# Two graph layers on one core: node rounds of phase B in turns of six, with two spilled rounds among four kept ones, and a ring of three products

## The reference, cut to what matters

```python
def _L0(node_feature, W_l, W_r, edge_index):           # mean over neighbours
    summed = segment_sum(node_feature[src], dst, n)
    agg = summed / maximum(deg, 1.0)[:, None]
    return agg @ W_l.T + node_feature @ W_r.T

def _L1(x, edge_index, edge_attr, W1, b1, g1, be1, W2, b2, g2, be2, W3, b3):
    agg = segment_sum(edge_attr, src, x.shape[0])
    h = concatenate([x, agg], axis=1)
    h = _bn(silu(h @ W1 + b1), g1, be1)                # batch norm over all nodes
    h = _bn(silu(h @ W2 + b2), g2, be2)
    return h @ W3 + b3

h = maximum(_layernorm(x), 0.0)
x = x + _L0(h, W_l, W_r, edge_index)
h = maximum(_layernorm(x), 0.0)
x = x + _L1(h, edge_index, edge_attr, W1, ...)
```

## Time and profile before

| | |
|---|---|
| median of 3 runs | 1533.28 us (1531.57 to 1533.95) |
| the profiled execution, reported time | 1530.96 us |
| its span, first to last instruction | 1529.2 us |
| busy: TensorE, VectorE, ScalarE, GpSimd | 69%, 72%, 57%, 55% |
| mean granted TensorE clock | 0.896 |
| DMA | 333.62 MB, 218 GB/s over the span |
| y loads, z stores of full rounds | 16 and 16, 512 KB each |
| scatter-adds of phase B | 196 |

### The profile page before, as it was taken

The page is one execution under the profiler, slowest core; times in us unless marked ns, Lnnn a source line. Parts: engine busy times, 40 slices in busy tenths (PEclk is TensorE's granted clock), DMA queues, the critical chain, the costliest instruction groups (busy, mean ns, idle before and its releaser), DMA issues.

```text
span 1529.2 us, 23466 instructions
## 1 busy us (share of the span) xinstructions
PE 1062.3 (69%) x5247; PEld 746.2 (49%) x5247; DVE 1101.3 (72%) x4641; ACT 868.1 (57%) x1686; POOL 836.9 (55%) x601
## 2 busy tenths in 40 slices
PE   3656776776656666637777777666666877997866
PEld 1235555665544444524444444444444765446765
DVE  6987777776556555538888888776753877778978
ACT  5956566656544544327666766655563545665533
POOL 6768888888888888657666667665652000000000
PEclk9989989889888978769999999998986998998989
DMA  9979889877666666557887778899986996306999
GB/s 278 386 250 225 218 216 216 192 163 159 146 146 146 145 145 143 120 137 188 194 197 192 194 193 201 238 259 257 265 231 198 354 326 229 136 27 235 407 403 372
DMA packets 231506, 333.62 MB, mean 218 GB/s; under 512 B 42106, under 2 KB 93394, under 8 KB 231444
## 3 DMA queue, kind: packets, MB, share of 16 engines
q1 hardware_dynamic: 157516, 285.22, 55.6%
q0 software_dynamic: 68864, 38.50, 20.3%
q10 hardware_dynamic: 5064, 9.29, 1.9%
HBM read 179.16 MB, written 153.71 MB: 218 GB/s over the span
## 4 chain that ended last, share of the span: by engine, by line
POOL 36%; DMA 26%; issue 15%; PE 12%; DVE 8%; SPq 1%; ACT 1%; DVEq 1%; POOLq 0%; ACTq 0%
POOL acc L808 20%; POOL acc L824 10%; DMA acc<-tabs,target_b 8%; DMA acc<-zT,target_b 8%; POOL xin L785 6%; PE ps L1494 6%; DMA zT<-x_dram 3%; DVE res L1088 2%; DMA xin<-acc 2%; PE ps L1504 2%; PE ps L1470 1%; PE ps L1473 1%; DVE zT L1342 1%; DVE zT L1346 1%; PE ps L1476 1%
## 5 line engine op out<-in xcount | busy, mean ns | idle before, releaser
L1390 PE MATMUL ps<-zT 128*128 128x512 f32 (+5 forms) x784 | 298.7, 536 | 206.7 <-ACT zT L924 133.2
L808 POOL DMA_INDIRECT acc<-zT,tabs x196 | 316.7, 1616 | 69.2 <-issue 58.5
L1390 PEld LDWEIGHTS ps<-zT 128*128 128x128 f32 (+1 forms) x784 | 172.7, 231 | 358.8 <-issue 197.4
L877 ACT ACTIVATE zT<-res,zT 128x128 f32<-128x128 f32 x398 | 158.5, 480 | 111.4 <-DVE zT L1167 111.4
L824 POOL DMA_INDIRECT acc<-zT,target_b x100 | 163.9, 1639 | 91.8 <-DMA acc<-tabs,target_b 30.5
L1125 DVE SCALAR_TENSOR_TENSOR zT<-zT 128x128 f32<-128x128 f32 (+3 forms) x392 | 193.2, 549 | 11.7 <-DMA zT<-row_dram 5.4
L824 POOL DMA_INDIRECT acc<-tabs,target_b x96 | 152.1, 1584 | 90.3 <-DMA acc<-tabs,target_b 31.2
L1193 DVE BATCH_NORM_STATS2 zT<-zT 128x6 f32<-128x128 f32 (+1 forms) x384 | 79.2, 279 | 164.8 <-DMA zT<-in_x_dram 164.5
L785 POOL DMA_INDIRECT xin<-in_x_dram,tabs x140 | 144.3, 1031 | 53.5 <-issue 42.1
L1382 PE MATMUL ps<-ident,zT 128*128 128x128 f32 (+1 forms) x784 | 118.4, 300 | 62.4 <-ACT zT L877 62.2
L1419 PE MATMUL ps<-wr,hT 128*128 128x128 f32 (+1 forms) x784 | 103.0, 286 | 53.2 <-DVE zT L1184 48.9
(11 more groups left out here) (148 smaller groups left out, 1959.7 us busy)
## 6 DMA issues: line engine op xcount, KB each, us to landing
acc<-bst SPq DMA_DIRECT2D x12, 2112.0 KB, 21.9
acc<-bst SPq DMA_DIRECT2D x48, 528.0 KB
zT<-row_dram SPq DMA_DIRECT2D x98, 256.0 KB, 5.6
zT<-in_x_dram SPq DMA_DIRECT2D x48, 512.0 KB, 6.8
zT<-acc SPq DMA_DIRECT2D x48, 512.0 KB, 4.3
x_dram<-res SPq DMA_DIRECT2D x48, 512.0 KB, 5.2
zT<-x_dram SPq DMA_DIRECT2D x42, 512.0 KB, 8.6
out_dram<-zT SPq DMA_DIRECT2D x42, 512.0 KB, 7.9
```

Of the source, the lines that this page charges most:

```text
L808: pool.indirect_dma_start(acc1, bass.IndirectOffsetOnAxis(ap=target_a[0:p, k, j:j + 1], axis=0), v[0:p, j, :], None, compute_op=ALU.add).t ...
L877: ins = nc.scalar.activation(to[0:p, c, :], t[0:p, c, :], ACT.Identity, bias=nm[0:p, par, k:k + 1], scale=rs[0:p, par, k:k + 1])
L1390: ins = nc.tensor.matmul(psA[:, 0:j + 1, 0:p], t[0:p, j, :], same[0:p, par, at:at + j + 1, 0:p], start=(j == ROWS - 1), stop=(j == 0))
```

## The change

Node rounds and edge rounds of B part ways. `place_b(g, m)` gives for step m of turn g (six steps a turn, eight turns) the node round: steps 2 and 5 take spilled rounds 32 + 2g and 33 + 2g, the other four take kept rounds 4g to 4g + 3. The edge round, the parity and all buffers go on by the step's number. `sweep_b` takes the place of `sweep` for B: the first turn and the last one with the tail are written out, the six between are one loop of six rounds. The number of slots falls from four to three, since six steps are a multiple of three, and the copy of a product waits for the scatter of three rounds back. The wait for a stored z moves from each spilled round to steps 1 and 4, which write the buffer next. The order of phases A, C, F and G stays.

```diff
+def three_ago(sem, par, i, inc=1):
+
+    return sem[1 - par], (i - 1 + par) * inc
...
     RING = 4
+    RING_B = 3
+    TURN = 6
+    TURNS = RF // TURN
...
-        vrow_b = [vrow[:, 1, :, :], vrow[:, 0, :, :], free_slots[0], free_slots[1]]
+        vrow_b = [vrow[:, 1, :, :], vrow[:, 0, :, :], free_slot]
...
+        def place_b(g, m):
+
+            spill = m % 3 == 2
+            node = 2 * KEPT + 2 * g + m // 3 if spill else 4 * g + m - m // 3
+            return 3 * g + m // 2, m % 2, False, spill, m % RING_B, node, g
+
+        def sweep_b(eng, body, wide=False):
+
+            def fixed(r):
+                if r == RF:
+                    return IT, 0, True, True, RF % RING_B, RF, TURNS
+                return place_b(r // TURN, r % TURN) if 0 <= r < RF else None
+
+            n = 4 if wide else 3
+
+            def peeled(lo, hi):
+                for r in range(lo, hi):
+                    body(*(fixed(r + k) for k in range(-1, n - 1)))
+
+            peeled(0, TURN)
+            with eng.Fori(1, TURNS - 1) as g:
+                near = [place_b(g - 1, TURN - 1)] + [place_b(g, m) for m in range(TURN)]
+                near += [place_b(g + 1, m) for m in range(2)]
+                for j in range(TURN):
+                    body(*near[j:j + n])
+            peeled(RF - TURN, RF + 1)
...
-            def load_b_nodes(i, par, tail, spill, *_):
-
-                r = 2 * i + par
+            def load_b_nodes(i, par, tail, spill, slot, node, g):
+
                 sp.wait_ge(*two_ago(B["added"], par, i))
-                load_nodes(aux[:, par, :, :], acc1_v, r, tail, B["a_loaded"][par])
+                load_nodes(aux[:, par, :, :], acc1_v, node, tail, B["a_loaded"][par])
                 if spill:
-                    load_nodes(xin[:, par, :, :], y_v, r, tail, B["y_loaded"][par])
+                    load_nodes(xin[:, par, :, :], y_v, node, tail, B["y_loaded"][par])
...
-                store_nodes(res[:, par, :, :], x1_v, 2 * i + par, tail, B["stored"][par])
+                store_nodes(res[:, par, :, :], x1_v, node, tail, B["stored"][par])
...
-            sweep(sp, step_b, (KEPT,), wide=True, margin=2)
+            sweep_b(sp, step_b, wide=True)
...
-                elif type(i) is int and i == 1:
+                elif type(i) is int and 2 * i + par < RING_B:
                     act.wait_ge(*this(s_sc1, 0, IT, 64))
                 else:
-                    act.wait_ge(*four_ago(s_sc2, par, i, 48))
-                    act.wait_ge(*four_ago(s_end2, par, i, 16))
+                    act.wait_ge(*three_ago(s_sc2, par, i, 48))
+                    act.wait_ge(*three_ago(s_end2, par, i, 16))
...
-                    for d, t in spilled(z_dram[2 * (i - KEPT) + par], hT[:, par, :, :], tail):
+                    for d, t in spilled(z_dram[node - 2 * KEPT], hT[:, par, :, :], tail):
...
-                if spill:
-                    act.wait_ge(B["z_stored"][par], (i - KEPT) * 16)
+                if not tail and not spill and slot == 1:
+                    if par == 0:
+                        act.wait_ge(B["z_stored"][par], (g + 1) * 16)
+                    elif type(g) is not int or g:
+                        act.wait_ge(B["z_stored"][par], g * 16)
...
-            sweep(act, body_b, (KEPT,), wide=True)
-            copy_z(IT, 0, True, 1)
+            sweep_b(act, body_b, wide=True)
+            copy_z(IT, 0, True, True, 0, RF, TURNS)
...
-                    dve.wait_ge(B["y_loaded"][par], (i - KEPT + 1) * 16 + (16 if tail else 0))
+                    dve.wait_ge(B["y_loaded"][par], (g + 1) * 16 + (16 if tail else 0))
...
-                y = xin[:, par, :, :] if spill else kept(i, par)
+                y = xin[:, par, :, :] if spill else held(node)
                 for c, q in chunk_parts(tail):
-                    deg = rdeg[0:q, bass.ds(r * CHUNKS + c, 1)]
+                    deg = rdeg[0:q, bass.ds(node * CHUNKS + c, 1)]
```

More of the change, by code:

```diff
@@ L90, in gnn_layers @@
     RING = 4
+    RING_B = 3
+    TURN = 6
+    TURNS = RF // TURN
+    assert TURNS * TURN == RF and TURNS * 4 == 2 * KEPT and TURN % RING_B == 0 and TURNS >= 3
     AHEAD = 4
@@ L149, in gnn_layers @@
         target_a = tabs[:, 5 * IC:6 * IC].bitcast(u32).rearrange("p (r j) -> p r j", j=ROWS)
-        free_slots = [tabs[:, k * GROUP:(k + 1) * GROUP].rearrange("p (j d) -> p j d", j=ROWS) for k in range(2)]
+        free_slot = tabs[:, 0:GROUP].rearrange("p (j d) -> p j d", j=ROWS)
         src_tab = sb("src_tab", [P, RF + 1, 2, ROWS])
@@ L426, in kept, with held @@
             return zT[:, 2 * i + par, :].rearrange("p (c q) -> p c q", q=P)
+        def held(node):
+            return zT[:, node, :].rearrange("p (c q) -> p c q", q=P)
         def place_a(i, par, late):
@@ L574, in step_b @@
             def step_b(before, now, after, ahead):
-                i, par, tail, spill, _ = now
+                i, par, tail, spill, slot, node, g = now
                 sp.wait_ge(*this(s_end2, par, i, 16))
@@ L589, in _ @@
             sp.wait_ge(*this(A["transposed"], 0, IT))
-            for par in range(2):
-                load_b_nodes(0, par, False, 0)
+            for m in range(2):
+                load_b_nodes(*place_b(0, m))
             for par in range(2):
                 load_b_edges(1, par, False, 0)
-            sweep(sp, step_b, (KEPT,), wide=True, margin=2)
+            sweep_b(sp, step_b, wide=True)
             sp.wait_ge(*this(s_sc2, 0, IT, 48))
@@ L825, in scatter_b @@
                         acc2, bass.IndirectOffsetOnAxis(ap=target_b[0:p, k, j:j + 1], axis=0),
-                        vrow_b[k % RING][0:p, j, :], None, compute_op=ALU.add)\
+                        vrow_b[k % RING_B][0:p, j, :], None, compute_op=ALU.add)\
                         .then_inc((s_end2 if j == ROWS - 1 else s_sc2)[par], 16)
@@ L957, in _, with copy_z @@
             sweep(act, body_a, (SPILLED, PRE))
-            def copy_z(i, par, tail, spill):
+            def copy_z(i, par, tail, spill, slot, node, g):
                 act.wait_ge(*this(B["product"], par, i))
                 for c, p in pieces(tail):
-                    z = hT[:, par, c, 0:p] if spill else kept(i, par)[:, c, 0:p]
+                    z = (hT[:, par, :, :] if spill else held(node))[:, c, 0:p]
                     ins = nc.scalar.activation(z, psQ[:, c, 0:p], ACT.Copy)
@@ L1429, in sum_edges_b, with multiply_edges_b @@
                 presum(rows[:, par, :, :], par, tail).then_inc(B["summed"][par], 1)
-            def multiply_edges_b(i, par, tail, _, slot):
+            def multiply_edges_b(i, par, tail, spill, slot, *_):
                 pe.wait_ge(*this(B["sum_copied"], par, i))
@@ L1434, in multiply_edges_b @@
                 first = type(i) is int and i == 0 and par == 0
-                edge_product(w1b, par, tail, None if first else vrow_b[(slot - 1) % RING]).then_inc(B["v_ready"][par], 1)
+                edge_product(w1b, par, tail, None if first else vrow_b[(slot - 1) % RING_B]).then_inc(B["v_ready"][par], 1)
             def round_b(before, now, after, ahead):
-                i, par, tail, spill, _ = now
+                i, par, tail = now[:3]
                 if ahead:
```

8 lines of the change are left out of this document (4 added, 4 removed).

## The result

The changed kernel takes 1547.51 us (median of 4 runs, 1544.13 to 1548.51) against 1533.53 us of the kernel before: a ratio of 1.009, 95% interval 1.0072 to 1.0108. It is slower by 14 us. The forecast was 1538 us, range 1520 to 1549.

What follows compares the result with a forecast made beforehand. Phase B was taken as bound by rounds of one DMA burst released by a scatter's landing, plus dead time. Order +5.6, end of B -1 and addresses +0.4 gave +5.0 us on 1533.28: 1538 us, range 1520 to 1549.

Steps and rivals of the forecast that it cites:

- the 43 periods: Phase B between the last-scatter landings (S) at 700.04 and 1126.62: 426.6 us before, 432.2 us forecast, +5.6.
- X: Period of a burst carrying y and z together in phase B, taken as 11.5 us, bounds 9.35 to 12.4.
- The order: Spreading spilled rounds in phase B: 14 double bursts at 11.5 us plus 29 plain periods, +5.6 us.
- The even value of 11.10: Double-burst period at which the 43 periods of phase B would take equal time: 14 X = 155.4 us.
- VectorE's loop: Phase B loops grow from four rounds to six, 246 VectorE instructions in place of 165; taken as 0 us.
- the third rival: VectorE's six-round loop reloads code at five jumps; at 6 us each 9 us on top, 1547 us; chance 0.12.
- The other loops: Engines compute node numbers from the turn's number; SyncE's steps before its first load bounded by 2.4 us, taken 0.4.
- The ring: Three product slots in place of four: ScalarE's copy is 11.6 us early, nothing reaches it, 0 us.
- The waits for stored z: Wait before the ReLU two rounds after, issued one body earlier: 9.35 us against a 3.6 us landing, 0 us.
- The end of B: After 1126.62 the z stores of rounds 45 and 46 are missing: -1 us (0 to -3).
- the first (costs add): Rival: y and z cost in a lone round their average in a row, X = 11.1, 1533 us; chance 0.23.
- The second (a lone double burst is absorbed): Rival: a double burst between plain ones is absorbed, X 10.0 to 10.6, time 1518 to 1526 us; chance 0.31.

Runs made afterwards that it cites:

- e3: The changed kernel's new order and three slots, phase B written out without loops on all engines; 43 periods 428.20 us, ratio 1.0014 to the kernel before.
- e2: The kernel before in its old order, with three product slots and phase B written out on all engines; 43 periods 420.02 us, ratio 0.9954.
- e4: The changed kernel with ScalarE's z copy and store ahead of the normalisation; 43 periods 443.95 us, ratio 1.0097 to the kernel before.
- e1: The changed kernel with VectorE's phase B written out, other engines in loops of six; 43 periods 432.85 us, ratio 1.0059 to the kernel before.
- e10: The changed kernel with SyncE, ScalarE and TensorE written out, VectorE alone in its loop of six; 43 periods 437.79 us, ratio 1.0061.
- e12: The kernel before, old order, with VectorE's phase B loops at six rounds a pass in place of four; 43 periods 428.06 us, ratio 1.0012.
- e5: The kernel before in its old order with its four product slots, phase B written out on all engines; 43 periods 420.29 us, ratio 0.9951.
- e13: The changed kernel run again with no edit; 43 periods 445.07 us, ratio 1.0078 to the kernel before.
- e8: New order, all written out, y loads left out and acc1 read in place of y; 43 periods 408.32 us, run once, 1504.87 us.
- e7: New order, all written out, y loaded one burst earlier, three rounds ahead; 43 periods 425.01 us, ratio 0.993 to the kernel before.
- e11: New order, all written out except SyncE, which alone has its loop of six; 43 periods 434.30 us, ratio 1.005 to the kernel before.

## Why the prediction came out as it did

The sign, the place and the range held; the size was a third of the measured one (+5 against +14). In the terms of the sum the 43 periods were to take 5.6 us more and took 16.1: X was 11.93 and not 11.5 (6.0 us), the last period was 12.31 and not a plain 9.35 (3.0 us), and the 28 other plain rounds took 1.7 us more. Point by point, by cause:

- **The order: +5.6 taken, +8.2 measured** (e3 - e2). The frame was right: bursts that follow the landing of a scatter, y and z together every third time, nothing gained by spreading. X was taken as 11.5 us; it is 11.93 with all loops, 11.24 without VectorE's and 11.09 with none. The even value of 11.10 was wrong: it counts the last period, 12.69 us, as a spilled round that turns into a plain one, and it stays long in either order (12.31). Without it the even value is (426.58 - 261.80 - 12.69) / 14 = 10.86, and z's price in a row is 0.50 us and not 0.65. The term also lacked the plain round behind a double burst, which costs 0.4 us more (9.49 against 9.11 in e3), 14 times. An X too high for the order alone (11.5 against 11.09) hid both in part; so the right sign of this term is in part luck.
- **Why X would be 11.5** was a wrong reason with a usable number. I had it that z costs by its distance from S. e4 moved it, and the cost moved with it into the burst before.
- **VectorE's loop: 0 taken, +9.9 and +9.6 measured** (e1, e10). This is the step that failed, and most of the miss. It stood as the third rival with 0.12, "decides once a jump costs more than the 4.2 us that VectorE has to spare". The pauses are 3.3 to 4.0 us, 3.6 on average, so by that rule they were covered. The 4.2 us were read in a plain round of the old order. There a pause costs little (e12: 1.5 us for all, within scatter). In the new order VectorE starts a body 8.1 to 10.6 us after S in every double burst, and catches up in the two rounds behind; that a pause takes this away and makes the next burst late is my reading, seen in one round and not in the average of the bursts that it should hit. The Trainium skill ("Runtime: NRT & Kernel Launch", Instruction fetch mechanics) states that a taken branch outside the two loaded 16 KiB pages stalls for a fetch. The traces fit that: with VectorE's loop of four rounds no pause over 0.7 us, with its loop of six one at each jump, and 15 and 16 packets on queue 14 that come and go with that loop (e1, e10). The fetch itself is not in the profile.
- **The other loops: +0.4 taken, -1.6 measured** (4.6 in e1 over e3, against 6.3 in the kernel before over e5). I took the difference alone and never asked what the loops cost that were there. This is where the time was to be had. By itself the -1.6 is within scatter.
- **The ring: 0 and 0** (e5 - e2 = 0.3 us). In the changed kernel no copy of a product waits for a landing; the waits of L937 are all for TensorE:

```profile
ACT tabs L937 <- PE ps L1440: 12.1, 13, 1.5
...
ACT zT L937 <- PE ps L1440: 3.5, 8, 0.7
```

- **The waits for stored z: 0, and none is seen**, though z lands in 7.0 us and not in 3.6.
- **The end of B: -1 taken, -3.3 measured** (-2.9 in e13: 37.1 against 40.0). Rounds 45 and 46 are kept now and have no z to store.

Sum: 8.2 + 9.9 - 1.6 - 0.3 for the ring = 16.1 us for the 43 periods. It is no check that this is what was measured, as the steps lead from the one kernel to the other over the same profiles; by the ratios the loop's share is smaller, 5 to 7 us. With the end of B the sum is 12.8, beside 14 us between the medians.

Of the rivals, the first (costs add) was nearest for y and z themselves: e8 and the profile of e7 show y paid at 1.4 to 1.6 us. It was wrong for the kernel: the order alone costs 8.2 us, and the loops changed too. The second (a lone double burst is absorbed) is out: double bursts average 11.93 us (11.74 in e13, where a single one of 10.37 is the shortest of all 28), and even the y of e7 without z takes 10.71. The single period of 10.02 on which it rested was one short one: the same first y alone took 10.92 in e2, 11.96 in e5 and 10.74 in e12. With it falls what I had put beside it, that the round-robin by packets of the Trainium skill ("DMA: Bandwidth & Descriptors") might let the scatters through: by the landings, 7.56 us in a double burst, they did not get through early.

## What to carry to other kernels

Where a phase runs in rounds whose transfers are all released by the landing of the last one, expect a transfer to cost about its own length in whatever round it lies: in this kernel spreading the heavy rounds gained nothing, and the rounds behind them paid a little more. Compare kinds of rounds only after the first and last ones, which have their own length, are set aside. Before a loop's body grows, look at what each engine counts in it, and read an engine's spare time in the rounds where the change will put the load, not in the quiet ones. And ask what the present loops cost: written out on all engines, phase B in the old order is faster than both kernels here, by 0.46% and 0.49% against the kernel before.

## What the runs showed of the hardware that I had not expected

VectorE's loop of six rounds pauses 3.3 to 4.0 us at each jump back and its loop of four 0.7 at most: 20.7 us of idle "issue" against 0.9 in the 43 periods. ScalarE with a loop of six has 0.2 us of such idle time, and 7.6 us in four waits where its rounds are written out (e3). TensorE has it with and without a loop (46.8 us in the changed kernel, 57.0 in e3), so nothing can be read from it there. What SyncE's loop costs, some 0.1 us a period on the queue that starts every burst, is the other surprise, as far as e11 shows it.
